# A two-layer gated network on one core: loops written out, weight blocks read backwards, preparation steps moved

## The reference, cut to what matters

```python
x = x + jnp.tanh(g_xattn[0]) * _L0_xattn_ref(ctx_1024, _layernorm(x), ...)   # a state-space scan
x = x + jnp.tanh(g_ffn[0]) * _L0_ffn_ref(_layernorm(x), L0_ffn_w1, L0_ffn_w2)
x = x + jnp.tanh(g_xattn[1]) * _L1_xattn_ref(_layernorm(x), ctx_1024, ...)   # softmax attention
x = x + jnp.tanh(g_ffn[1]) * _L1_ffn_ref(_layernorm(x), L1_ffn_proj1, ...)

def step(state, inp):                       # the scan: 512 channels, 16 states each
    d, b, c, u = inp
    dA = jnp.exp(d[..., None] * A)
    state = state * dA + (d * u)[..., None] * b[:, None, :]
    y = jnp.einsum('bdn,bn->bd', state, c)
    return (state, y)

def _bitlinear(x, w):                       # both products of the first network
    rms = jax.lax.rsqrt(jnp.maximum(jnp.mean(w * w), EPS))
    w_quant = jnp.clip(jnp.round(w * rms), -1.0, 1.0) / rms
    scale = 127.0 / jnp.maximum(jnp.max(jnp.abs(x), axis=-1, keepdims=True), EPS)
    x_quant = jnp.clip(jnp.round(x * scale), -128.0, 127.0) / scale
    return jnp.einsum('bsd,fd->bsf', x_quant, w_quant)
```

## Time and profile before

| | us |
|---|---|
| median of 3 runs (1029.64 to 1030.63) | 1030.56 |
| profiled execution's own time | 1030.36 |
| its span, first to last instruction | 1028.5 |
| busy PE / DVE / ACT / POOL | 811.7 / 807.4 / 683.1 / 562.1 |
| chain of waits: PE, DVE, issue, ACT, POOL, DMA | 38%, 17%, 15%, 11%, 8%, 5% |
| `u<-work` transfers, 120 of 512 KB | 6.2 to land |
| `ring<-ffn_dram`, 144 of 256 KB | 4.9 to land |

### The profile page before, as it was taken

How to read it: one execution, slowest core, us unless ns; L and a number is a source line. 1 busy time by engine, 2 the same in 40 slices (tenths; PEclk the granted TensorE clock), 3 DMA queues, 4 the chain that set the end, 5 groups by cost and what they waited for, 6 DMA issues and landing times.

```text
span 1028.5 us, 10874 instructions
## 1 busy us (share of the span) xinstructions
PE 811.7 (79%) x2668; PEld 398.4 (39%) x2704; DVE 807.4 (78%) x937; ACT 683.1 (66%) x1004; POOL 562.1 (55%) x477
## 2 busy tenths in 40 slices
PE   5431222489889998989699989889799989888998
PEld 2110010244343443444243434344343434445887
DVE  3879977877888998787998997878988997664333
ACT  4578969567479984567489974665599863723442
POOL 0298687113699885133999883134998881322000
PEclk9555555599989999999899999999899999998999
DMA  8059996000159998121089997301299984200321
GB/s 283 0 103 206 227 221 115 8 1 2 41 121 237 217 249 213 51 83 41 10 181 236 226 225 184 102 3 41 51 210 208 240 203 130 103 0 21 103 96 69
DMA packets 51439, 130.07 MB, mean 126 GB/s; under 512 B 6304, under 2 KB 7456, under 8 KB 50864
## 3 DMA queue, kind: packets, MB, share of 16 engines
q0 software_dynamic: 17280, 62.92, 33.1%
q1 hardware_dynamic: 34096, 66.53, 18.7%
HBM read 62.33 MB, written 4.19 MB: 65 GB/s over the span
## 4 chain that ended last, share of the span: by engine, by line
PE 38%; DVE 17%; issue 15%; ACT 11%; POOL 8%; DMA 5%; DVEq 1%; ACTq 0%; POOLq 0%
PE bank L616 8%; PE bank L629 8%; DVE pair L1218 6%; DMA u<-work 5%; PE bank L644 4%; POOL work L1646 4%; PE pair L644 4%; PE pair L554 4%; ACT pair L837 3%; ACT L837 3%; PE pair L507 2%; DVE work L1223 1%; DVE fst L1469 1%; PE bank L465 1%; PE bank L450 1%
## 5 line engine op out<-in xcount | busy, mean ns | idle before, releaser
L1646 POOL TENSOR_TENSOR work<-du,bcast 128x1024 f32<-128x1024 f32 x128 | 350.6, 2756 | 46.6 <-DVE du L1269 46.0
L1218 DVE TENSOR_TENSOR_SCAN pair<-pair,work 128x512 f32<-128x512 f32 x256 | 299.2, 1214 | 30.3 <-ACT pair L837 26.4
L837 ACT ACTIVATE pair<-dt,a_neg 128x512 f32<-128x512 f32 x256 | 165.4, 680 | 37.9 <-DVE work L1223 35.2
L616 PE MATMUL bank<-stage,ring 128*128 128x512 f32 x384 | 173.8, 595 | 6.0 <-ACT bcast L822 4.4
L1223 DVE TENSOR_TENSOR work<-pair,ccast 128x1024 f32<-128x1024 f32 x128 | 156.8, 1225 | 17.6 <-DVE pair L1218 9.5
L1657 POOL DMA_DIRECT2D u<-work x120 | 127.4, 1062 | 55.8 <-DMA u<-work 22.7
L416 PE MATMUL bank<-xd,pick 128*128 128x512 bf16 x112 | 51.2, 457 | 102.1 <-ACT bcast L822 63.0
L616 PEld LDWEIGHTS bank<-stage,ring 128*128 128x128 f32 x384 | 70.8, 190 | 82.3 <-issue 75.2
L629 PE MATMUL bank<-ring,stage 128*128 128x512 f32 x192 | 91.9, 624 | 12.6 <-DVE stage L1521 10.7
L416 PEld LDWEIGHTS bank<-xd,pick 128*128 128x128 bf16 x128 | 13.1, 102 | 160.8 <-ACT bcast L822 96.9
L507 PE MATMUL pair<-w1q,qT 128*128 128x512 bf16 x244 | 58.9, 388 | 6.3 <-ACT qT L1044 5.8
(11 more groups left out here) (179 smaller groups left out, 1549.7 us busy)
## 6 DMA issues: line engine op xcount, KB each, us to landing
u<-work POOLq DMA_DIRECT2D x120, 512.0 KB, 6.2
ring<-ffn_dram SPq DMA_DIRECT2D x144, 256.0 KB, 4.9
ring<-ffn_dram SPq DMA_DIRECT2D x16, 512.0 KB, 3.3
xres<-x_dram SPq DMA_DIRECT2D x4, 1024.0 KB, 5.4
stage<-w_dram SPq DMA_DIRECT2D x1, 4096.0 KB, 17.0
stage<-w_dram SPq DMA_DIRECT2D x4, 1024.0 KB, 7.2
out_dram<-stage SPq DMA_DIRECT2D x16, 256.0 KB, 2.5
ctxT<-ctxT_dram SPq DMA_DIRECT2D x4, 512.0 KB, 7.3
```

The costliest lines, as they stand in the source:

```text
L616: last = pe.matmul(banks[2 + f % 2][:], piece(f)[:, k * P:(k + 1) * P], xnT[:, k, :], start=k == 0, stop=k == J - 1)
L837: act.activation(pairs[s % DECAYBUFS][:, q, :], dt[:, p * HALF + q, :], ACT.Exp, scale=a_neg[:, p * HALF + q, n:n + 1]).then_inc(s_decay, 1)
L1218: dve.tensor_tensor_scan(pair[:, q, :], pair[:, q, :], rows[:, q, :], 0.0, ALU.mult, ALU.add).then_inc(s_scan, 1)
L1646: pool.tensor_tensor(work[:, s % SCANBUFS, :, :], du[:, p * HALF:(p + 1) * HALF, :], bcast[:, n % 2, :].unsqueeze(1).broadcast_to([P, HALF ...
```

## The change

The three loops over the full passes (and SP's over two) become Python loops, so each pass is written out with constant counts. The second round of down products takes the blocks from 15 to 0: the last eight of the first round stay in the ring, so 40 blocks are loaded a pass instead of 48, and places alternate in direction from batch to batch. The steps of the first network's preparation get other slots; the last six go behind the scan (`W_LATE`), after the last attention copy and ahead of `turning`. On all four compute engines calls in `between`, `turning` and `closing` change places.

```diff
@@ -51,13 +51,13 @@
-W_MEAN = {5: 0, 10: 1}
-W_STEPS = {(4, 0): ("square", 0, 0), (4, 1): ("square", 0, 1), (4, 2): ("square", 0, 2), (5, 0): ("square", 0, 3),
-           (6, 0): ("scale", 0, 0), (6, 1): ("sign", 0, 0), (6, 3): ("scale", 0, 1), (7, 0): ("sign", 0, 1),
-           (7, 2): ("scale", 0, 2), (7, 3): ("sign", 0, 2), (8, 1): ("scale", 0, 3), (8, 2): ("sign", 0, 3),
-           (8, 3): ("square", 1, 0), (9, 0): ("square", 1, 1), (9, 1): ("square", 1, 2), (9, 3): ("square", 1, 3),
-           (10, 2): ("scale", 1, 0), (10, 3): ("sign", 1, 0), (11, 0): ("scale", 1, 1), (11, 1): ("sign", 1, 1),
-           (11, 2): ("scale", 1, 2), (11, 3): ("sign", 1, 2), (12, 0): ("scale", 1, 3), (12, 1): ("sign", 1, 3)}
+W_MEAN = {6: 0, 11: 1}
+W_STEPS = {(4, 1): ("square", 0, 0), (4, 3): ("square", 0, 1), (5, 1): ("square", 0, 2), (5, 3): ("square", 0, 3),
+           (6, 3): ("scale", 0, 0), (7, 0): ("sign", 0, 0), (7, 1): ("scale", 0, 1), (7, 2): ("sign", 0, 1),
+           (7, 3): ("scale", 0, 2), (8, 0): ("sign", 0, 2), (8, 1): ("scale", 0, 3), (8, 3): ("sign", 0, 3),
+           (9, 1): ("square", 1, 0), (9, 3): ("square", 1, 1), (10, 1): ("square", 1, 2), (10, 3): ("square", 1, 3),
+           (12, 0): ("scale", 1, 0), (12, 1): ("sign", 1, 0)}
+W_LATE = (("scale", 1, 1), ("sign", 1, 1), ("scale", 1, 2), ("sign", 1, 2), ("scale", 1, 3), ("sign", 1, 3))
 ATT_BANKS = (4, 6, 7, 6)
...
@@ -186,8 +186,23 @@
-        def piece(k):
-            return ring[:, k % PIECES, :]
+        def place(b, k):
+            n = k if k < 2 * FT else PIECES - 1 - (k - 2 * FT)
+            return n % PIECES if b % 2 == 0 else PIECES - 1 - n % PIECES
+        def piece(b, k):
+            return ring[:, place(b, k), :]
+        def loaded(b, k):
+            return s_piece[place(b, k)], (b * (LOADS // PIECES) + k // PIECES + 1) * 16
+        def down_load(r, f):
+            if r == 0:
+                return FT + f
+            return 2 * FT - 1 - f if f < PIECES else 2 * FT + f - PIECES
...
@@ -339,13 +354,17 @@
-                used = k - PIECES
-                if used >= FT:
-                    sp.wait_ge(s_fmm2, b * 2 * FT + used - FT + 1)
-                elif used >= 0:
-                    sp.wait_ge(s_fmm1, b * FT + used + 1)
-                weights = ffn_d[k][:, 0:D] if k < FT else ffn_d[k % FT][:, D:2 * D]
-                sp.dma_start(piece(k), weights).then_inc(s_piece[k % PIECES], 16)
+                if k >= 2 * FT:
+                    sp.wait_ge(s_fmm2, b * 2 * FT + FT + k - 2 * FT + 1)
+                elif k >= FT + PIECES:
+                    sp.wait_ge(s_fmm2, b * 2 * FT + k - FT - PIECES + 1)
+                elif k >= PIECES:
+                    sp.wait_ge(s_fmm1, b * FT + k - PIECES + 1)
+                elif b:
+                    sp.wait_ge(s_fmm2, (b - 1) * 2 * FT + FT + PIECES + k + 1)
+                weights = ffn_d[k][:, 0:D] if k < FT else ffn_d[k - FT][:, D:2 * D] if k < 2 * FT else \
+                    ffn_d[PIECES - 1 - (k - 2 * FT)][:, D:2 * D]
+                sp.dma_start(piece(b, k), weights).then_inc(loaded(b, k)[0], 16)
...
@@ -539,8 +558,8 @@
                 q_transposes(m, (2,))
+                q_transposes(m, (3,))
                 up1(m, 1, (FC - 1,))
-                q_transposes(m, (3,))
...
@@ -623,10 +642,11 @@
                         pe.wait_ge(s_fgelu, b * FT + FT)
-                k = FT + r * FT + f
-                pe.wait_ge(s_piece[k % PIECES], (b * (LOADS // PIECES) + k // PIECES + 1) * 16)
+                k = down_load(r, f)
+                block = f if r == 0 else FT - 1 - f
+                pe.wait_ge(*loaded(b, k))
                 for t in (2 * r, 2 * r + 1):
-                    last = pe.matmul(banks[2 + t % 2][:], h_tile(f)[:, t * P:(t + 1) * P], piece(k),
+                    last = pe.matmul(banks[2 + t % 2][:], h_tile(block)[:, t * P:(t + 1) * P], piece(b, k),
                                      start=f == 0, stop=f == FT - 1)
...
@@ -701,11 +721,11 @@
                 up1(b, 3, range(FC - 1))
+                norm_transpose(b, 0)
                 down1(b, 1)
-                norm_transpose(b, 0)
-                low_rank(m)
                 up1(b, 3, (FC - 1,))
                 transpose_h(b, 2)
+                low_rank(m)
                 norm_transpose(b, 1)
...
@@ -715,12 +735,12 @@
                 attend(b, 1, m)
+                attend(b, 2)
                 norm_transpose(b, 3)
-                attend(b, 2)
                 scan_bcast(m, 1, 0)
+                scan_bcast(m, 0, 1)
                 norm_transpose(b, 4)
                 attend(b, 3)
-                scan_bcast(m, 0, 1)
                 norm_transpose(b, 5)
...
@@ -802,7 +822,7 @@
             pass_(None, rest=False)
-            with pe.Fori(0, B - 1) as i:
+            for i in range(0, B - 1):
                 pass_(i)
...
@@ -1074,8 +1094,8 @@
                 q_scale(m, 0)
+                q_scale(m, 1)
                 q_copy(m, (0,))
-                q_scale(m, 1)
                 gelu1(m, 0, range(FC - 2))
...
@@ -1083,8 +1103,8 @@
                 q_copy(m, (2,))
+                q_copy(m, (3,))
                 gelu1(m, 1, (FC - 1,))
-                q_copy(m, (3,))
...
@@ -1151,6 +1171,9 @@
                 att_copy(m, prev, J - 1)
+                if not rest:
+                    for step in W_LATE:
+                        weight(*step)
                 turning(m)
...
@@ -1304,21 +1329,21 @@
                 h_scale(b, 0)
+                h_scale(b, 1)
+                h_quant(b, 0)
                 convolve(m, 0)
                 convolve(m, 1)
-                h_quant(b, 0)
-                h_scale(b, 1)
+                h_quant(b, 1)
                 convolve(m, 2)
-                h_quant(b, 1)
+                convolve(m, 3)
                 second(b, 0)
-                convolve(m, 3)
                 h_scale(b, 2)
+                h_quant(b, 2)
                 second(b, 1)
-                h_quant(b, 2)
                 h_scale(b, 3)
                 h_quant(b, 3)
+                split(m)
                 second(b, 2)
-                split(m)
                 softplus_max(m)
...
@@ -1349,8 +1374,8 @@
                 weight_low(0)
+                weight_low(1)
                 norm_apply(b, 4)
-                weight_low(1)
                 third(b, 1)
...
@@ -1393,12 +1418,12 @@
                 first_sum(m, 1)
+                first_sum(m, 2)
                 q_norm(m, 0)
-                first_sum(m, 2)
+                q_norm(m, 1)
                 q_out(m, 0)
-                q_norm(m, 1)
+                q_out(m, 1)
                 first_sum(m, 3)
-                q_out(m, 1)
                 q_norm(m, 2)
...
```

More of the change, by code:

```diff
@@ L35 @@
 PIECES = 8
-LOADS = 3 * FT
+LOADS = 2 * FT + PIECES
 PAD = TAPS - 1
@@ L398, in _ @@
             load_context(1)
-            with sp.Fori(0, B - 2) as i:
+            for i in range(0, B - 2):
                 run(i, True, True)
@@ L613, in f_up @@
                     pe.wait_ge(s_xnTc, b * 2 * T + 2 * T)
-                pe.wait_ge(s_piece[f % PIECES], (b * (LOADS // PIECES) + f // PIECES + 1) * 16)
+                pe.wait_ge(*loaded(b, f))
                 for k in range(J):
-                    last = pe.matmul(banks[2 + f % 2][:], piece(f)[:, k * P:(k + 1) * P], xnT[:, k, :],
+                    last = pe.matmul(banks[2 + f % 2][:], piece(b, f)[:, k * P:(k + 1) * P], xnT[:, k, :],
                                      start=k == 0, stop=k == J - 1)
@@ L1161, in weight_step, with weight @@
                 if (slot, quarter) in W_STEPS:
-                    kind, i, c = W_STEPS[slot, quarter]
-                    (square if kind == "square" else scale if kind == "scale" else quantise)(i, c)
+                    weight(*W_STEPS[slot, quarter])
+            def weight(kind, i, c):
+                (square if kind == "square" else scale if kind == "scale" else quantise)(i, c)
             def set_up():
@@ L1201, in _ @@
             pass_(None, rest=False)
-            with act.Fori(0, B - 1) as i:
+            for i in range(0, B - 1):
                 pass_(i)
@@ L1418, in turning @@
                 first_sum(m, 2)
+                q_out(m, 1)
                 first_sum(m, 3)
                 q_norm(m, 2)
-                q_out(m, 1)
                 q_norm(m, 3)
+                fourth(b, 1)
                 q_out(m, 2)
-                fourth(b, 1)
                 q_out(m, 3)
@@ L1571, in _ @@
             pass_(None, rest=False)
-            with dve.Fori(0, B - 1) as i:
+            for i in range(0, B - 1):
                 pass_(i)
@@ L1603, in between @@
                 h_round(b, 1)
+                h_round(b, 2)
                 norm(b, 0)
-                h_round(b, 2)
                 norm(b, 1)
@@ L1768, in _ @@
             pass_(None, rest=False)
-            with pool.Fori(0, B - 1) as i:
+            for i in range(0, B - 1):
                 pass_(i)
```

14 lines of the change are left out of this document (7 added, 7 removed).

## The result

The kernel after takes 1014.64 us (median of 4, 1011.89 to 1014.99), the kernel before 1030.53 beside it: ratio 0.9841 [0.9825, 0.9858]. That is 16 us less; 11.8 were forecast. The time lies in the range, and near the lower end of the forecast's own (1013 to 1024). The profiled execution took 1014.47 us, its span is 1012.7. One of e4's six executions (1032.59 us at a mean clock of 0.854, where the others had 0.893 to 0.899) and one of the kernel before (2945.47 us) are left out of e4's median and of all ratios.

What follows compares the result with a forecast made beforehand. First scan bound by DVE with holes mostly from ScalarE, full passes' packed scan by a ScalarE-TensorE ring left unshortened. 1030.4 us with -3.5 - 7 + 4.1 - 2.7 - 2.2 - 0.5 = -11.8 gives 1018.6; range 1013 to 1024, with rivals 1008 to 1027.

Steps and rivals of the forecast that it cites:

- Start of the first scan: First network's weight steps in new slots shorten DVE's holes of 3.79 and 2.05 us: 3.5 us less, bounds 1.8 and 5.8.
- The 6.53 us stall: Late first scan: moving POOL's statistic and its first use removes DVE's hole; 7 us less net, bounds 3.5 and 10.
- the rival of the transfers: First scan: accumulations' landing or POOL's queue bound it once ScalarE's stalls go; about 1024 us, chance 0.17 with POOL.
- POOL then has it some two half-steps before ScalarE asks; the wait goes: Late first scan: statistic in slot 11, first use at (12,0), so ScalarE's 6.95 us wait for it disappears.
- Late steps: First turning: three scales and three signs, 12.1 us, partly covered by ScalarE's idle 7.07; net 4.1 more, bounds 2.5 and 6.
- Back edges: Seams between full passes: writing loops out removes two branches at 1.35 us each; 2.7 us less, bounds 0 and 5.4.
- The chain: Turning's products to POOL's softplus step: 48.93 us in the first full pass, 50.28 in the second, pricing a branch at 1.35.
- Register instructions: In front of waits, hidden under the Gelu or DVE's previous product; removing them gives nothing, up to 1 us in all.
- Order in the full passes: Earlier quantisation and low-rank product fill TensorE's waits; net 0.75 us a pass, 2.2 less for three.
- Loads backwards: Down weights in the full passes: 24 loads, 6.3 MB fewer, gain nothing; at most 1.9 us a pass.
- Closing: `weight_low(1)` fills the 0.72 us in which DVE waits for POOL: 0.5 us less.
- The rival of code streaming: Full passes: exposed code fetches cost about 2.7 us each, slower at six or more, 1037.5 us at seven; chance 0.07.

Runs made afterwards that it cites:

- e4: Kernel after, but 48 loads a pass with the second round of down weights forward as before; 1012.83 us, ratio 0.9838.
- e9: e4 with the first full pass written out and the second and third in a loop on each engine; 1015.64 us, ratio 0.9867.
- e5: e4 with each compute engine's three full passes in one-trip loops of their own; 1013.09 us, ratio 0.9842.
- e8: Kernel after with the old order of calls in `between` on all engines; 1019.47 us, ratio 0.9901.
- e7: Kernel after without the six late steps, so three quarters of the second network's weights stay unscaled and unsigned; 1010.69 us, ratio 0.9816.
- e2: Kernel before with only the weight preparation steps laid out as after, slots and late block; 1025.57 us, ratio 0.9969.
- e6: Kernel after with the second row's first scale and sign one quarter later, the scale behind the third attention copy; 1010.62 us, ratio 0.9803.
- e1: Kernel before with only its loops over the full passes written out on every engine; 1025.39 us, ratio 0.9962.
- e3: Kernel before with only the new order of calls on the four engines, loops and weights kept; 1026.44 us, ratio 0.9966.
- e10: e6 with VectorE's list of the first turning as in the kernel before; 1012.02 us, ratio 0.9823.

## Why the prediction was right, and where it was wrong

- **Start of the first scan, -3.5: right.** The holes of 3.79 and 2.05 became one of 1.89: 3.95 less.
- **The 6.53 us stall, -7: right in size.** Half-step 30 is 2.32 us late on POOL, forecast 2. The scan gave 9.7 of 10.5. The size is only good to some 3 us: with the same code in the first scan, e9, e5, e8 and e7 took 121.26, 121.40, 122.01 and 122.41 us where after, e4 and e2 took 124.2 to 124.4. In e9 and e4 POOL's products start at the same times, counted from the first scan instruction, up to 93 us of the span. Then accumulations issued between 99 and 108 us land in 7.0 to 7.1 us in e9 and in 7.1 to 9.3 in e4. POOL falls behind, and DVE stands 2.53 and 1.30 us for its products in e4, 0.64 and 0.38 in e9. So the rival of the transfers has a part here; why the same transfers land later stays open.
- **"POOL then has it some two half-steps before ScalarE asks; the wait goes": the step that failed.** I moved the statistic's slot and left out what then stands before it in POOL's queue. POOL had no lead left by then (its products release the scan at 127.61, 136.11 and 166.26 us); the 5.4 us of gates' statistics, which I had as a cost to the scan, stand before the weights' statistic too. The 6.32 us that were left held the attention copy, 2.5 us on the path. e6, which lets the copy go first, gets 1.4 of them back.
- **Late steps, +4.1: measured +4.07, right.** I had the block 5.0 late and about 0.9 given back. The first `q_scale` starts 9.98 us after the row sum instead of 5.08, 4.9 later. From it to the first q copy it is 1.96 instead of 2.79, 0.8 given back, since DVE has done the next sum meanwhile. e2 shows both without the new order. Up to the fourth copy the loss is 3.75 in the kernel after, and 4.4 to 5.0 in e4, e5, e8 and e9, which have the same code there. In the full passes the row sum to the first q copy is 7.96 in both kernels.
- **Back edges, -2.7: right, by the evidence that was named.** e9 has 1.45 a branch, 2.9 for two. The chain had 1.35, and in the kernel before this difference appears at the seam. ScalarE's first copy in the first and second full pass:

```profile
215.22 0.60 ACT L861 ACTIVATE xpad<-bank 128x512 f32<-128x512 f32 x1 [1.49 <-PE bank L442]
...
438.96 0.60 ACT L861 ACTIVATE xpad<-bank 128x512 f32<-128x512 f32 x1 [2.48 <-PE bank L442]
```

  12 us behind the fourth q copy the second pass is 1.34 us later than the first, the third 1.31, and both stay so up to the softplus step. In e1, without branches, this gap is 1.18 us in the first and the second pass, and DVE's first step behind it is not later at all. By the Trainium skill (Runtime: NRT & Kernel Launch, Instruction fetch mechanics), a taken branch to code outside the window stalls the engine for a fetch; the trace agrees as far as the gap on ScalarE is 2.5 us longer in e9, of which the path sees 1.45. But e1 shows a trap: its second pass too is 1.2 us longer than its first up to the softplus step (45.11 against 43.90). There the difference comes late, in the last 5 us, in a stretch of 12 us in which the clock was lower, 0.86 in the first pass and 0.72 in the second:

```profile
247.40:259.40 12.00, 11.82 (x40) 5.29 (x39) 9.16 (x17) 11.64 (x14) 3.79 (x4) 0.86 0.05 11
467.33:479.33 12.00, 11.67 (x36) 4.88 (x35) 7.74 (x15) 10.43 (x12) 3.79 (x4) 0.72 0.00 0
```

- **Register instructions, "nothing, up to 1 us in all": a term mis-sized.** 0.7 us a pass, 2.1 in all. They were said to run under the Gelu and under the previous product; in the packed half of the scan, 0.8 of 112.5 us did not.
- **Order in the full passes, -2.2: mis-sized by half or more.** 4.6 alone (e3), 7.0 in the written-out kernel (e8). The waits I named, 3.06 us, are the ones that went, and the Gelu wait that I set against them is there (0.90). What I took off beyond that, no run shows.
- **Loads backwards, nothing: right** (e4). The Trainium skill (DMA: Bandwidth & Descriptors, Issuing engines are not separate DMA queues) has all transfers share the DMA engines; the trace agrees as far as an accumulation lands in 6.0 us instead of the 6.2 of the kernel before and of e4, but no time that can be measured came of it.
- **Closing, -0.5: not seen.** DVE's wait for POOL at that step fell from 0.72 to 0.44; the next steps have 0.72 and 1.06 instead of 0.44 and 1.05. The closing and tail took 145.0 to 147.1 us in all kernels, with the old closing (before, e1, e2) as with the new, so 0.5 can't be told there.
- **The rival of code streaming** had its threshold one fetch too high: five fetches of 2.7 us are 13.5, more than the 11.8 gained.
- **The clock: a term I didn't have.** The three full passes together, us:

| | loops | written out |
|---|---|---|
| old order | 669.7 (before) | 663.9 (e1) |
| new order | 665.1 (e3) | 657.0 (after), 654.9 (e4) |

  Writing out alone gives 5.8, the order alone 4.6, both 12.7 (14.8 in e4). So 2.3 to 4.3 us come only together. Registers (2.1) and branches (2.9) make 5.0 of what writing out gives; it gives 5.8 in the old order and 8.1 in the new. The passes written out and in the new order come at 218.0 to 219.0 or at 219.7 to 220.7 us; in the longer ones the low clock falls into the stretches before the scan. The rest lies between the fourth q copy and the first up product, where the clock's mean differs too (0.66 to 0.72 in the last stretch of the kernel before, 0.85 after). That the clock makes all of the rest is argued and not shown.

## What to carry to other kernels

When a small step is moved on one engine, write down the whole queue of the engine that feeds it, with its lead at that moment: moving the user by a half-step or two doesn't remove its wait if the producer then stands behind 5 us of other work. A median time to landing can hide a stretch in which transfers take half as long again; read it for the stretch in question. Lists of two engines that hand rows to each other must be changed together, and separately for the pass where a block of extra work stands between them. Before two passes are compared to price one event in between, put their granted clocks side by side, stretch by stretch, and find the instruction at which the difference first appears.

## What was not expected of the hardware

- The same code runs in passes of 218.5 and 220.7 us on one TensorE: mean granted clocks 1.00 and 0.96 before the scan, and 0.85 and 0.72 at its start, between the 1.2 and 2.4 GHz levels. TensorE had been busy 40.59 of 42.26 and 41.27 of 42.73 us in the stretch ahead. A low clock at the scan's start alone doesn't make a pass long: e10's first has 0.73 there and takes 218.29. What decides which it is no run shows, but an edit can win or lose 2 us a pass beside its own effect.
- Register instructions ahead of waits are never busy time in the profile, yet cost 0.7 us in a pass of 221 us, where two passes with the same clocks are compared.
- The first scan varied by 3.2 us with the same code (121.26 to 124.43), and the difference starts with accumulations that land later.
- Eight blocks of weights less, 2.1 MB a pass, in stages that had the DMA engines 96 to 100% busy, changed no time that can be measured.
